# Attention of a fused kernel: exponentials and maxima of neighbouring chunks merged, fold by four transposes with its sum on GpSimd

## What is computed

```python
def _L1_attn_ref(hidden_states, Wq, Wk, Wv, Wo):
    H, HKV, D = (16, 4, 64)
    ...
    q = _apply_rope(q, cos, sin)
    k = _apply_rope(k, cos, sin)
    G = H // HKV
    qg = q.reshape(b, HKV, G, s, D)
    scale = jnp.float32(D) ** (-0.5)
    scores = jnp.einsum('bkgqd,bkpd->bkgqp', qg, k) * scale
    causal = jnp.tril(jnp.ones((s, s), dtype=bool))
    scores = jnp.where(causal, scores, jnp.float32(-1e+30))
    probs = jax.nn.softmax(scores, axis=-1)
    out = jnp.einsum('bkgqp,bkpd->bkgqd', probs, v).reshape(b, H, s, D)
    out = out.transpose(0, 2, 1, 3).reshape(b, s, H * D)
    return out @ Wo
```

## Time and profile before

| | us |
|---|---|
| median of three runs | 5142.48 |
| lowest and highest run | 5138.14, 5155.52 |
| the profiled execution | 5132.4 |
| its span | 5130.6 |
| busy in it: PE, DVE, ACT, POOL | 4350.8, 3699.7, 2826.4, 1743.6 |
| first scores product and last one of attention | 1961.2, 3783.1 |

### The profile page before, as it was taken

The page is one execution under the profiler, slowest core; times in us unless marked ns, Lnnn a source line. Parts: engine busy times, 40 slices in busy tenths (PEclk is TensorE's granted clock), DMA queues, the critical chain, the costliest instruction groups (busy, mean ns, idle before and its releaser), DMA issues. The chain is left out here.

```text
span 5130.6 us, 83669 instructions
## 1 busy us (share of the span) xinstructions
PE 4350.8 (85%) x20410; PEld 3061.4 (60%) x20411; DVE 3699.7 (72%) x7521; ACT 2826.4 (55%) x6543; POOL 1743.6 (34%) x1517
## 2 busy tenths in 40 slices
PE   6877887779999776999999999999986649999960
PEld 2333333346666335888888888888866537777740
DVE  6999999966666556888888888888864433333349
ACT  6777777522222005888888888888853324444420
POOL 5777777610000002121211212121127753333321
PEclk8999999999999998999999999999998869999985
DMA  1000000021111433011210201021035435545558
GB/s 42 13 13 13 13 13 9 9 74 37 38 36 36 168 128 89 26 50 30 54 51 26 58 25 51 26 58 51 25 97 175 168 119 160 155 150 159 154 171 276
DMA packets 323976, 389.89 MB, mean 76 GB/s; under 512 B 118721, under 2 KB 257337, under 8 KB 317899
## 3 DMA queue, kind: packets, MB, share of 16 engines
q1 hardware_dynamic: 250827, 270.27, 17.3%
q0 software_dynamic: 26112, 73.44, 4.0%
q10 hardware_dynamic: 46944, 45.16, 3.2%
HBM read 235.51 MB, written 153.24 MB: 76 GB/s over the span
## 5 line engine op out<-in xcount | busy, mean ns | idle before, releaser
L1524 DVE TENSOR_TENSOR probsT<-ps_t,probsT 128x512 fp32r<-128x512 f32 (+3 forms) x1280 | 779.2, 609 | 136.7 <-ACT probsT L1464 115.8
L1299 PE MATMUL ps_s<-kbuf,qbuf 128*128 (+1 forms) x2602 | 766.8, 379 | 73.2 <-POOL qbuf L1409 36.4
L1464 ACT ACTIVATE probsT<-ps_t 128x512 fp32r<-128x512 f32 (+3 forms) x1280 | 685.3, 535 | 257.2 <-PE ps_t L1312 233.6
L1456 ACT ACTIVATE probs<-ps_s,negm 128x512 f32<-128x512 f32 (+3 forms) x1297 | 811.4, 626 | 27.4 <-DVE negm L1517 26.5
L1324 PE MATMUL ps_o<-probsT,vbuf 128*128 128x512 f32 (+3 forms) x2560 | 815.6, 402 | 6.8 <-ACT folding L1470 6.3
L1504 DVE TENSOR_REDUCE pmax<-ps_s 128x1 f32<-128x512 f32 (+3 forms) x1301 | 777.0, 600 | 46.9 <-PE ps_s L1299 22.9
L1312 PE MATMUL ps_t<-idn,probs 128*128 128x128 f32 x4352 | 695.5, 275 | 13.8 <-DVE probsT L1524 13.8
L445 POOL TENSOR_TENSOR dBx<-u,b_all 128x1024 f32<-128x1024 f32 x256 | 615.6, 2407 | 237.6 <-DVE h L531 226.9
L1312 PEld LDWEIGHTS ps_t<-idn,probs 128*128 128x128 f32 x4352 | 517.8, 142 | 134.5 <-DVE probsT L1524 40.9
L1299 PEld LDWEIGHTS ps_s<-kbuf,qbuf 128*128 128x128 f32 x2602 | 444.7, 189 | 192.2 <-issue 78.6
L1407 POOL CAST qbuf<-qstage 128x512 fp32r<-128x512 f32 x132 | 82.8, 627 | 1271.7 <-DMA qstage<-q_scr 774.6
(11 more groups left out here) (248 smaller groups left out, 7239.9 us busy)
## 6 DMA issues: line engine op xcount, KB each, us to landing
xr<-xs ACTq DMA_DIRECT2D x294, 136.0 KB, 2.2
parts<-y SPq DMA_DIRECT2D x36, 1024.0 KB, 5.2
qstage<-q_scr SPq DMA_DIRECT2D x264, 128.0 KB, 2.9
w_gu<-W_guT SPq DMA_DIRECT2D x64, 384.0 KB
q_scr<-rot SPq DMA_DIRECT2D x64, 256.0 KB
attn<-ostage SPq DMA_DIRECT2D x128, 128.0 KB, 2.0
at<-attn SPq DMA_DIRECT2D x32, 512.0 KB
w_d<-W_downT SPq DMA_DIRECT2D x64, 192.0 KB
```

Source lines behind the costliest of these rows:

```text
L1299: last = nc.tensor.matmul(ps_s[:, u % RING, 0:w], qbuf[:, BAND * s + j, :], kbuf[:, bass.ds(kslot, 1), part, c * CW:c * CW + w], start=par ...
L1456: nc.scalar.activation(probs[:, k, at:at + n, :], ps_s[:, u % RING, 0:n * P], ACT.Exp, bias=negm[:, tile, :], accum_out=sums[:, s, j, c:c ...
L1464: nc.scalar.activation(probsT[:, g % SLOTS, 0, lo:], ps_t[:, t % 2, lo:], ACT.Copy).then_inc(high_t.sem, 1)
L1524: nc.vector.tensor_tensor(probsT[:, g % SLOTS, 1, lo:], ps_t[:, t % 2, lo:], probsT[:, g % SLOTS, 0, lo:].bitcast(F32), ALU.subtract).then ...
```

## The change

Exponentials and maxima of two neighbouring chunks of a tile become one instruction over two banks of ps_s, where the first is not the tile's diagonal chunk and the two banks are neighbours. A table, MERGE, has for each slot either nothing, a single chunk, or a pair; a pair is done where its second chunk stood, and then counts two on exp_done or cmax. Places that a merged maximum or sum no longer fills hold a constant from two memsets. The fold becomes four plain transposes of 128x128. ACT copies them to SBUF (spill, into halves), which frees the bank of ps_t, and GpSimd adds the halves and multiplies with the reciprocals (finish); DVE's normalise goes. t_out is split into low_t (DVE), spilled (ACT) and n_done (GpSimd). The stacked identities go, and with them two small DMAs. GpSimd's queries for the next head are split in two parts that stand among the four finish steps. The mask stays as it is. LEAD, AHEAD and RING are unchanged.

```diff
@@ chunk, MERGE, span
+    MERGE = []
+    for k in range(NU):
+        ends, v = [None] * STEPS, 0
+        while v < STEPS:
+            s, j, c = CHUNKS[k][v]
+            two = c < s and (k * STEPS + v) % RING < RING - 1
+            ends[v + two] = (v, 1 + two)
+            v += 1 + two
+        MERGE.append(ends)
+
+    def span(k, v):
+
+        (first, count), (s, j, c) = MERGE[k][v], CHUNKS[k][v]
+        bank = (k * STEPS + first) % RING
+        return bank * CW, bank * CW + (count - 1) * CW + blocks(s, j, c) * P
...
+    def before_use(k, t):
+
+        k, t = (k, t - k * TURNS - 2) if t - k * TURNS >= 2 else (k - 1, t - k * TURNS - 2 + TURNS)
+        if t == TURNS - 1 or t == FOLD[k] + 1:
+            return "fold", 2 * k + (t == TURNS - 1) + 1
+        return "turn", k * STEPS + t - (t > FOLD[k]) + 1
...
-        ps_s = pb("ps_s", [P, RING, CW])
+        ps_s = pb("ps_s", [P, RING * CW])
-        pmax = sb("pmax", [P, 2 * BAND, BANDS])
+        pmax = sb("pmax", [P, NU, 2 * BAND, BANDS])
+        halves = sb("halves", [P, 2, BAND, 2, HD])
+        whole = sb("whole", [P, BAND, HD])
-        NCONST = 4
+        NCONST = 2
@@ sync
-                            sp.wait_ge(t_out.sem, t_out.at(hx, fold_use(k, short) + 1))
+                            sp.wait_ge(n_done.sem, n_done.at(hx, 2 * k + short + 1))
@@ tensor
+            def bank_free(hx, k, t):
+                kind, count = before_use(k, t)
+                if kind == "fold":
+                    pe.wait_ge(spilled.sem, spilled.at(hx, count))
+                else:
+                    pe.wait_ge(low_t.sem, low_t.at(hx, count))
...
                 for j in range(BAND):
-                    last = nc.tensor.matmul(ps_t[:, t % 2, j * HD:(j + 1) * HD], folding[:, j * P:(j + 1) * P], idn_2[:, :],
-                                            start=True, stop=True)
+                    last = nc.tensor.transpose(ps_t[:, t % 2, j * P:(j + 1) * P], folding[:, j * P:(j + 1) * P], idn[:, :])
                 last.then_inc(f_done.sem, 1)
@@ gpsimd
+            def finish(hx, n):
+                s, half = QUEUE[n], halves[:, n % 2, :, :, :]
+                after(spilled.sem, spilled.at(hx, n + 1))
+                after(n_done.sem, n_done.at(hx, n))
+                nc.gpsimd.tensor_tensor(whole[:, :, :], half[:, :, 0, :], half[:, :, 1, :], ALU.add).then_inc(added.sem, 1)
+                after(added.sem, added.at(hx, n + 1))
+                after(r_done.sem, r_done.at(hx, n + 1))
+                after(o_out[s].sem, o_out[s].at(hx - 1))
+                nc.gpsimd.tensor_tensor(ostage[:, BAND * s:BAND * (s + 1), :], whole[:, :, :],
+                                        rinv[:, s, :, :].to_broadcast((P, BAND, HD)), ALU.mult).then_inc(n_done.sem, 1)
+
+            def head(hx):
+                next_queries(hx, 0)
+                finish(hx, 0)
+                finish(hx, 1)
+                next_queries(hx, 1)
+                finish(hx, 2)
+                finish(hx, 3)
@@ scalar
             def exps(hx, k, v):
-                s, j, c = CHUNKS[k][v]
-                u = k * STEPS + v
+                if MERGE[k][v] is None:
+                    return
+                first, count = MERGE[k][v]
+                s, j, c = CHUNKS[k][first]
...
-                nc.scalar.activation(probs[:, k, at:at + n, :], ps_s[:, u % RING, 0:n * P], ACT.Exp, bias=negm[:, tile, :],
-                                     accum_out=sums[:, s, j, c:c + 1]).then_inc(exp_done.sem, 1)
+                nc.scalar.activation(probs[:, k, at:at + (hi - lo) // P, :].rearrange("p n t -> p (n t)"), ps_s[:, lo:hi], ACT.Exp,
+                                     bias=negm[:, tile, :], accum_out=sums[:, s, j, c:c + 1]).then_inc(exp_done.sem, count)
...
+            def spill(hx, k, short):
+                n, t = 2 * k + short, fold_use(k, short)
+                act.wait_ge(f_done.sem, f_done.at(hx, n + 1))
+                act.wait_ge(added.sem, added.at(hx, n - 1))
+                nc.scalar.activation(halves[:, n % 2, :, :, :], ps_t[:, t % 2, :], ACT.Copy).then_inc(spilled.sem, 1)
...
                         if v == FOLD[k] - 1:
                             take(hx, k, 0)
+                        if v == FOLD[k] + 1:
+                            spill(hx, k, 0)
                     next_exps(STEPS)
                     take(hx, k, 1)
+                    spill(hx, k, 1)
@@ vector
             def peak(hx, k, v):
+                if MERGE[k][v] is None:
+                    return
...
-                nc.vector.reduce_max(pmax[:, tile, c:c + 1], ps_s[:, u % RING, 0:blocks(s, j, c) * P],
-                                     axis=mybir.AxisListType.X).then_inc(cmax.sem, 1)
+                nc.vector.reduce_max(pmax[:, k, tile, c:c + 1], ps_s[:, lo:hi], axis=mybir.AxisListType.X).then_inc(cmax.sem, count)
...
-            def normalise(hx, k, short):
...
+            nc.vector.memset(pmax[:, :, :, :], -3.0e38).then_inc(blanked.sem, 1)
+            nc.vector.memset(sums[:, :, :, :], 0.0).then_inc(blanked.sem, 1)
```

More of the change, by code:

```diff
@@ L1296, in scores @@
                 w = blocks(s, j, c) * P
+                at = u % RING * CW
                 pe.wait_ge(exp_done.sem, exp_done.at(hx, u - RING + 1))
                 for part in range(2):
-                    last = nc.tensor.matmul(ps_s[:, u % RING, 0:w], qbuf[:, BAND * s + j, :],
+                    last = nc.tensor.matmul(ps_s[:, at:at + w], qbuf[:, BAND * s + j, :],
                                             kbuf[:, bass.ds(kslot, 1), part, c * CW:c * CW + w],
@@ L1302, in scores @@
                 if c == s:
-                    last = nc.tensor.matmul(ps_s[:, u % RING, w - P:w], idn_r[:, :], mask_r[:, :], start=False, stop=True)
+                    last = nc.tensor.matmul(ps_s[:, at + w - P:at + w], idn_r[:, :], mask_r[:, :], start=False, stop=True)
                 last.then_inc(s_done.sem, 1)
+            def bank_free(hx, k, t):
[4 more added lines that the diff above has]
+                    pe.wait_ge(low_t.sem, low_t.at(hx, count))
             def turn(hx, k, g):
@@ L1415, in set_values, with next_queries @@
                 nc.gpsimd.tensor_copy(vbuf[:, b, :, :], vnext[:, b, :, :].bitcast(F32)).then_inc(v_set.sem, 1)
[L1417 to L1421, removed]
+            def next_queries(hx, k):
+                after(s_done.sem, s_done.at(hx, (k + 1) * STEPS))
+                for n in (2 * k, 2 * k + 1):
+                    queries(hx + 1, n)
+            def finish(hx, n):
[15 more added lines that the diff above has]
+                finish(hx, 3)
             nc.gpsimd.memset(blank[:, :, :], 0.0).then_inc(blank_set.sem, 1)
@@ L1435, in _ @@
                 values(g + 1)
[L1436 to L1440, removed]
-                    set_values(g + 1, n)
+                finish(g * GROUP, 0)
+                finish(g * GROUP, 1)
+                next_queries(g * GROUP, 1)
+                finish(g * GROUP, 2)
+                finish(g * GROUP, 3)
+                with pool.Fori(1, GROUP - 1) as j4:
+                    head(pool.snap(g * GROUP + j4))
+                end = pool.snap(g * GROUP + GROUP - 1)
+                next_queries(end, 0)
+                finish(end, 0)
+                finish(end, 1)
+                next_queries(end, 1)
+                for n in range(2):
+                    after(pv_done.sem, pv_done.at(end, V_USED[n]))
+                    set_values(g + 1, n)
+                finish(end, 2)
+                for n in range(2, BANDS):
+                    after(pv_done.sem, pv_done.at(end, V_USED[n]))
+                    set_values(g + 1, n)
+                finish(end, 3)
         @block.scalar
@@ L1445, in exps @@
             def exps(hx, k, v):
-                s, j, c = CHUNKS[k][v]
-                u = k * STEPS + v
+                if MERGE[k][v] is None:
+                    return
+                first, count = MERGE[k][v]
+                s, j, c = CHUNKS[k][first]
                 tile = BAND * (s == UNITS[k][1]) + j
-                n = blocks(s, j, c)
-                if v == 0:
+                lo, hi = span(k, v)
+                if first == 0:
                     act.wait_ge(t_done.sem, t_done.at(hx - 1, (k + 1) * STEPS))
@@ L1498, in peak @@
             def peak(hx, k, v):
[L1500 to L1501 removed]
+                if MERGE[k][v] is None:
+                    return
+                first, count = MERGE[k][v]
+                s, j, c = CHUNKS[k][first]
                 tile = BAND * (s == UNITS[k][1]) + j
[L1503 to L1505 removed]
+                lo, hi = span(k, v)
+                dve.wait_ge(s_done.sem, s_done.at(hx, k * STEPS + v + 1))
+                nc.vector.reduce_max(pmax[:, k, tile, c:c + 1], ps_s[:, lo:hi], axis=mybir.AxisListType.X).then_inc(cmax.sem, count)
             def settle(hx, k, v):
```

39 lines of the change are left out of this document (18 added, 21 removed).

## The result

| | us |
|---|---|
| changed kernel, median of 4 runs (5741.12 to 5752.55) | 5748.69 |
| kernel before, median of 4 runs beside it | 5140.31 |
| ratio, 95% interval | 1.1175 [1.1154, 1.1196] |
| profiled execution of the changed kernel, its span | 5752.45, 5750.7 |

The change costs 608 us (5748.69 - 5140.31). The forecast was +571, a median of 5,714, with a range up to 5,815.

What follows compares the result with a forecast made beforehand. PE was taken to bound the kernel, 1.36 us a slot. Per head 18.7 - 1.3 + 0.8 + 0.1 - 0.5 = +17.8 us, times 32 = +570, plus 1.5: +571, median 5,714 us, range 5,540 to 5,815.

Steps and rivals of the forecast that it cites:

- The closed chain: Per pair, transposes, ACT's copy, exponential, scores, next transposes: 2.97 us instead of 1.36, 1.61 us of new wait.
- The pairs' term: New waits of the 13 merged exponential pairs in each head, after corrections: +18.7 us a head.
- the width: Extra time of a 1024-column exponential over a 512-column one before PE is let go: 0.42 us a pair.
- The fold: Four plain transposes on PE replace four products run as eight passes: -1.3 us a head; unit ends +0.1.
- The second turn behind the fold: After the second unit's first fold, the bank waits for ACT's copy: 2.0 us instead of 1.18, +0.8 a head.
- Waits that fall away: A third of PE's present idle time of 1.6 us a head goes: -0.5 us a head.
- Merged maxima at zero: DVE's merged maxima neither cost nor gain time, since PE's own 1.36 us a slot covers them.
- The third rival: PE's pauses at the pairs make its granted clock fall: 6,300 to 7,460 us; chance 2%.
- Hidden pairs: Rival: the pairs' wait is covered and only gains on PE count, 104 us less, 5,038 us; chance 4%.
- Two banks at double cost: Rival: an exponential reading two banks runs like two, +0.44 us a pair, 5,897 us; chance 4%.
- The pairs wait, but less: Rival: engines recover between pairs, so half of the 18.7 us a head comes, 5,415 us; chance 4%.
- Ordinary slots shrink: Rival: DVE and ACT set the 1.36 us slot; their relief saves up to 0.2 us in 27 slots, 5,541 us; 3%.

Runs made afterwards that it cites:

- e1: Kernel before, with paired exponentials issued at the second one's slot but as two single instructions; maxima and fold as before: 5606.39 us, ratio 1.0903.
- e8: Changed kernel with nothing merged, only the new fold, and ACT's copy of the first fold moved ahead of its copy of the transposes: 5113.74 us, ratio 0.9959.
- e4: Changed kernel with nothing merged, only the new fold with ACT's copy and GpSimd's sum: 5140.11 us, ratio 0.9984.
- e7: Changed kernel with its merged exponentials, but all maxima single: 5745.27 us, ratio 1.1184.
- e3: Changed kernel with single exponentials; merged maxima and the new fold stay: 5200.94 us, ratio 1.0104.
- e5: Changed kernel with pairs in the first unit alone (6 of 13), the second unit's exponentials and maxima single: 5387.93 us, ratio 1.0483.
- e2: Changed kernel with each merged exponential issued at its first member's slot instead of its second: 5288.7 us, ratio 1.0283.

## Why the prediction was right, and where it wasn't

- **The closed chain.** The step that carried the forecast held in every link, within 0.03 us where the same chunk widths stand (one pair runs from 3158.62 to 3161.59, the forecast 2.97). The last link varies with the scores between, 0.40 to 0.70 in one head against 0.57 for all. The pairs' term was +18.7 us a head; measured at full clock it is 74.23 - 56.20 = +18.0.
- **Place, not width.** The prediction gave 0.42 of 1.61 us to the width. e1 shows the rest, 13.0 us of 18.0 a head, without a single merged instruction.
- **The fold.** Forecast -1.3 + 0.1 for PE and the unit ends: three folds at 0.42 each. Measured at the unit ends -0.36 and -0.41, and about -0.16 at the first unit's fold (2.20 to 2.04 us from transposes to transposes): -0.9. The fourth, with a pair behind it, was priced at about +0.3 with its pair; it went from 2.59 to 2.90 us.
- **The second turn behind the fold.** Forecast 2.0 us in place of 1.18, measured 1.89 (1.87 in the changed kernel), with ACT's copy as the releaser. Right, and e8 showed that it was the order of two copies.
- **Waits that fall away.** -0.5 a head was a guess between bounds. In e4 PE idles 9.2 of 200 us (3000 to 3200) where it idled 5.8 before, and ACT's waits for maxima stand at 27.8 us, as before (26.5). Nothing fell away: zero. Together the last three terms were -0.9 a head and came to about -0.2, while the pairs' term was 0.7 too high; that the sum of 17.8 lies so close to 17.88 is luck: two errors of 0.7 cancel.
- **Merged maxima at zero.** Right in the changed kernel (e7), wrong as a statement on DVE's slot: "PE's own 1.36 us covers it" looked at the subtraction behind the maximum and not at the tile maximum three slots on. Without the pairs' chain it costs 61 us (e3).
- **The clock.** The third rival got the kind of thing right and its size wrong. The prediction said that the granted clock stays at 1.00 through pauses of this length; it dips once in most heads. The sign that it named for this rival, a clock under 1.00 in the stage, came without the rival's time: the dips cost some 28 us, not 584 or more. With the prologue's 5.7 they are the terms that the sum left out, 34 us of the 37 by which it was low.
- **The rivals.** Hidden pairs: no row speaks for it; the chain is there 13 times a head. Two banks at double cost: 1.107 us for 1024 columns, against 1.1 taken. The pairs wait, but less: 18.0 of 18.7 came, and e5 shows no recovery in between. Ordinary slots shrink: 1.36 to 1.39 us stays, even in the slot at 3208.04, where ACT and DVE have less than a microsecond of work each. By the Trainium skill (TensorE: Matmul & The Clock Gate, Back-to-back issue gap) 512-column matmuls with their weight loads follow each other by about 131 ns; the trace does not agree: two f32 products of 512 columns took 0.71 us (3208.40) where one alone takes 0.40, so they follow each other by some 0.3.

## What to carry to other kernels

In a loop in which several engines are full, look at an instruction's place in its engine's queue before its length; here the place cost 13 us a head and the length about 5. Merging two instructions delays the first one's result to the second one's place, and if a ring has no bank to spare, that delay can close a chain of waits through several engines. Price such a merge link by link, from the release of one slot to the release of the next. Ask of every "hidden" cost what hides it, and whether that cover is there without the rest of the change.

## What the runs showed of the hardware

- The granted clock fell to 1.2 GHz inside a running loop, for a part of 10 us, once in most heads, and cost 1.04 us in the early heads and 0.9 in the later ones. PE had been busy 3.90 and then 3.12 of 5 us ahead of and around the fall (rows above). Four heads of e1 with such falls took 73.4 us in place of 69.4. In the windows of 200 us the kernel before and e2 show 1.00 throughout, e1 1.00 until 3400 us and then 0.95 and 0.97, the changed kernel 0.97 to 0.99. Why the clock falls at that place, and why not in every head, stays open.
- The first transposes of the changed kernel took 1.06 us for four at 1.2 GHz, 0.60 at 2.4 GHz.
- An exponential over two PSUM banks costs no more than its columns: 1107 ns for 1024, 1006 for 896, 787 for 640, 684 for 512. A maximum likewise, 1217 ns for 1024 and 684 for 512: merging two saves 0.15 us of 1.37.
- GpSimd adds 128x256 with two halves from SBUF in 729 ns and multiplies with a broadcast factor in 613, both over the 600 that a quarter of the earlier trace rows gave.
